# An attention and feed-forward kernel: output bias and three high halves on GpSimd in the last part, instead of bias matmuls and VectorE

## The reference

```
x = x + xattn(layernorm(x), ctx, ctx, wq, wk, wv, wo)     # 16 heads of 16: correlation by FFT over the
                                                          # head, the best lags, softmax, rolled v, @ wo
x = x + ffn(layernorm(x), W_in, b_in, W_out, b_out)

ffn:  W_in_sim  = W_in  rounded to 8 bits, a scale per column
      W_out_sim = W_out rounded to 8 bits, a scale per row
      x_sim     = x rounded to 16 bits, one scale for the whole tensor
      hidden    = gelu(x_sim @ W_in_sim + b_in)           # 1024 wide
      hidden_sim= hidden rounded to 16 bits, one scale for the whole tensor
      out       = hidden_sim @ W_out_sim + b_out
```

## Time and profile before

| | |
|---|---|
| median of the timed runs | 1077.34 us |
| the profiled execution | 1077.55 us, span 1075.8 us |
| TensorE busy | 1055.1 us, 98% |
| VectorE busy | 970.5 us, 90% |
| ScalarE busy | 936.8 us, 87% |
| GpSimd busy | 504.6 us, 47%, nearly all before 595 us |
| granted TensorE clock | 1.00 |

### The profile page before, as it was taken

The page is one execution under the profiler, slowest core; times in us unless marked ns, Lnnn a source line. Parts: engine busy times, 40 slices in busy tenths (PEclk is TensorE's granted clock), DMA queues, the critical chain, the costliest instruction groups (busy, mean ns, idle before and its releaser), DMA issues.

```text
span 1075.8 us, 29041 instructions
## 1 busy us (share of the span) xinstructions
PE 1055.1 (98%) x9358; PEld 779.8 (72%) x9358; DVE 970.5 (90%) x2798; ACT 936.8 (87%) x1697; POOL 504.6 (47%) x674
## 2 busy tenths in 40 slices
PE   9999999999999999999998999999999999999998
PEld 7788887887888888888886444444444888888886
DVE  4889989989889889889899999999997999999998
ACT  5888888998999998888888788888888999999996
POOL 5788887888888888888887300000000000000000
PEclk9999999999999999999999999999999999999999
DMA  5445343343444334334441499999989899999995
GB/s 167 129 149 143 120 119 119 119 119 119 119 128 130 119 119 120 119 119 119 119 126 43 167 313 312 313 303 300 300 303 372 323 342 329 353 335 351 337 344 198
DMA packets 141521, 222.59 MB, mean 207 GB/s; under 512 B 72416, under 2 KB 92256, under 8 KB 137312
## 3 DMA queue, kind: packets, MB, share of 16 engines
q1 hardware_dynamic: 140320, 220.12, 62.0%
q10 hardware_dynamic: 1088, 1.05, 0.3%
HBM read 121.00 MB, written 83.89 MB: 190 GB/s over the span
## 4 chain that ended last, share of the span: by engine, by line
PE 53%; DVE 11%; issue 8%; DMA 3%; ACT 2%; DVEq 1%; ACTq 0%; POOL 0%; SPq 0%; POOLq 0%
PE bank L612 21%; DVE arena L1482 6%; PE bank L441 5%; PE bank L454 5%; PE bank L492 4%; PE bank L516 4%; PE bank L466 3%; PE bank L504 3%; PE bank L478 3%; PE bank L533 3%; DMA arena<-x_scratch 2%; DVE arena L1475 2%; DVE arena L1497 2%; PE bank L643 1%; DMA out<-arena 1%
## 5 line engine op out<-in xcount | busy, mean ns | idle before, releaser
L643 PE MATMUL bank<-wout,arena 128*128 128x256 f16 x2048 | 235.5, 273 | 2.7 <-DVE arena L1475 0.7
L643 PEld LDWEIGHTS bank<-wout,arena 128*128 128x128 f16 x2048 | 195.7, 98 | 44.2 <-DVE arena L1482 13.2
L612 PE MATMUL bank<-arena,win 128*128 128x512 f16 x1024 | 221.3, 379 | 1.1 <-DVE arena L1430 0.9
L612 PEld LDWEIGHTS bank<-arena,win 128*128 128x128 f16 x1024 | 100.0, 98 | 122.4 <-issue 1.4
L1482 DVE SCALAR_TENSOR_TENSOR arena<-arena,wout_rel 128x512 f16<-128x512 int16 x256 | 183.0, 746 | 3.9 <-ACT arena L912 1.3
L869 ACT ACTIVATE arena<-bank,b_in_sb,z_scale 128x512 f32<-128x512 f32 x192 | 147.1, 778 | 15.1 <-PE bank L612 10.0
L733 ACT ACTIVATE arena<-arena 32x128 f32<-32x128 f32 x256 | 78.5, 307 | 52.7 <-DVE arena L1186 50.4
L663 ACT ACTIVATE arena<-bank 128x512 f32<-128x512 f32 (+1 forms) x196 | 115.4, 590 | 6.4 <-PE bank L441 3.0
L905 ACT ACTIVATE arena<-arena,one 128x1536 int16<-128x1536 f32 x64 | 100.2, 1568 | 17.5 <-DVE arena L1482 15.3
L663 ACT ACTIVATE arena<-arena 128x512 f16<-128x512 f32 x192 | 113.0, 618 | 1.5 <-POOL arena L972 0.9
L1449 DVE TENSOR_REDUCE hmax_all<-arena 128x1 f32<-128x1024 f32 x96 | 111.3, 1210 | 2.9 <-ACT arena L869 2.9
(11 more groups left out here) (130 smaller groups left out, 2057.3 us busy)
## 6 DMA issues: line engine op xcount, KB each, us to landing
hidden_scratch<-arena SPq DMA_DIRECT2D x32, 1536.0 KB, 5.5
arena<-hidden_scratch SPq DMA_DIRECT2D x64, 768.0 KB, 7.1
arena<-in_ctx_turned SPq DMA_DIRECT2D x64, 256.0 KB, 2.7
arena<-in_x_turned SPq DMA_DIRECT2D x64, 256.0 KB, 2.7
arena<-in_x SPq DMA_DIRECT2D x64, 256.0 KB, 3.6
x_scratch<-arena SPq DMA_DIRECT2D x64, 256.0 KB, 3.5
arena<-x_scratch SPq DMA_DIRECT2D x32, 512.0 KB, 6.2
out<-arena SPq DMA_DIRECT2D x32, 512.0 KB, 4.0
```

The lines of the kernel that those rows point to most:

```text
L612: last = nc.tensor.matmul(bank[f][:, :].rearrange("p (n t) -> p n t", n=4), win16[:, f, c, :], xt[q % 3][:, s, :, c, :], start=s == 0 and ...
L643: last = nc.tensor.matmul(bank[m * 2 + k // 2][:, k % 2 * D:(k % 2 + 1) * D], gbuf[:, s, f, k * P:(k + 1) * P], wout16[:, f, :], start=f = ...
```

## The change

- **Bias.** The two bias matmuls of each quad and all of GpSimd's preparation go (with a few columns of the constant table). GpSimd adds the bias itself to x1 once that is loaded: `add_bias(q)`, one addition over 128x1024 f32.
- **High halves.** GpSimd makes those of f = 2, 4 and 6, ScalarE those of 1, 3, 5 and 7, VectorE that of 0 alone. GpSimd's order in quad q is: high 2, add_bias(q-1), high 4, high 6.
- **Additions.** The two PSUM banks of a quad are declared as one tensor of 1024, and `finish` is one instruction after the rest of f = 4; for the last quad it is two, each with a store of its own. It waits for add_bias as well.
- **Third x1 buffer**, in room of `store_x` that the first part used. SyncE loads x1 of quad q+1 after the store of q-1 is issued. The loops on SyncE and VectorE are written out for all quads.
- **Scale chains.** The three dependent instructions of each weight's scale are put in three successive steps, and what follows them moves two steps later (ScalarE's `weights`, the transposition of W_in).

```diff
-HIGH_ON_ACT = (1, 3, 5, 6, 7)
-FINISH_AFTER = {4: 0, 6: 1}
+HIGH_ON_ACT = (1, 3, 5, 7)
+HIGH_ON_POOL = (2, 4, 6)
+FINISH_AFTER = 4
...
-        yq = cut(2, 1024, ("p (k) -> p k", {}))
+        yq = cut(2, 1024, ("p (k) -> p k", {})) + [store_x[:, 0:1024]]
...
+        sums = [ctx.enter_context(nc.psum_tensor(f"sums{n}", [P, 1024], F32)) for n in range(2)]
+        bank = [sums[n // 2][:, n % 2 * 512:n % 2 * 512 + 512] for n in range(4)]
...
-                    if f == FC - 1:
-                        pe.wait_ge(S["bias_ready"], 1)
-                        for j in range(2):
-                            last = nc.tensor.matmul(bank[m * 2 + j][:, :].rearrange("p (b d) -> p b d", b=2), y_rows, bias_rows.unsqueeze(1).broadcast_to([P, 2, D]),
-                                                    start=False, stop=True, skip_group_check=True)
...
+            bias = b_out_sb[:, :].unsqueeze(1).broadcast_to([P, 4, D])
+            def add_bias(q):
+                pool.wait_ge(s_x1_ld[q % 3], 16 * (q // 3 + 1))
+                y = yq[q % 3].rearrange("p (b d) -> p b d", b=4)
+                nc.gpsimd.tensor_tensor(y, y, bias, ALU.add).then_inc(S["y_biased"], 1)
+            def high(q, f):
...
+                pool.wait_ge(S["c_hq"], q * 3 + (sum(f >= b for _, b in PARTS_OF_F) + 1))
+                wait(pool, S["c_f"], (q - 1) * FC + (f + 1))
+                nc.gpsimd.tensor_scalar(gbuf[:, 0, f, :], hq[:, f, :], wout_rel[:, f:f + 1], None, ALU.mult).then_inc(S["c_hi_pool"], 1)
+            for q in range(QUADS):
+                for f in HIGH_ON_POOL[:1]:
+                    high(q, f)
+                if q > 0:
+                    add_bias(q - 1)
+                for f in HIGH_ON_POOL[1:]:
+                    high(q, f)
+            add_bias(QUADS - 1)
...
+            def finish(q, part, parts):
+                n = 1024 // parts
+                of = slice(part * n, (part + 1) * n)
+                dve.wait_ge(S["y_biased"], q + 1)
+                dve.wait_ge(S["c_f"], (q + 1) * FC)
+                V.scalar_tensor_tensor(yq[q % 3][:, of], sums[q % 2][:, of], y_scale, yq[q % 3][:, of],
+                                       ALU.mult, ALU.add).then_inc(S["c_out"], 1)
...
                 if n == FC:
-                    scales(win_max, win_up).then_inc(S["w_in_scaled"], 1)
+                    floor_w(win_max, FC)
+                if n == FC + 1:
+                    invert_w(win_max, win_up, FC + 1)
+                if n == FC + 2:
+                    scale_w(win_up, FC + 2).then_inc(S["w_in_scaled"], 1)
```

More of the change, by code:

```diff
@@ L41 @@
 C_TURN = C_HD + HD
-C_ROW = C_TURN + 1
-C_ALL = C_ROW + 6
+C_ALL = C_TURN + 1
 W_UP = 64.0
@@ L253, in xattn_ffn_kernel @@
         s_x1_st = [sem(f"s_x1_st{n}") for n in range(2)]
-        s_x1_ld = [sem(f"s_x1_ld{n}") for n in range(2)]
+        s_x1_ld = [sem(f"s_x1_ld{n}") for n in range(3)]
         s_h_st = [sem(f"s_h_st{n}") for n in range(2)]
@@ L257, in xattn_ffn_kernel @@
         s_xt = [sem(f"s_xt{n}") for n in range(3)]
-        s_out = [sem(f"s_out{n}") for n in range(2)]
+        s_out = [sem(f"s_out{n}") for n in range(3)]
         def wait(eng, s, n):
@@ L358, in load_hidden, with load_x1, store @@
                 sp.dma_start(hidden_in[n], rows(h_dram, q)[:, part * 1536:(part + 1) * 1536]).then_inc(s_h_ld[n], 16)
[L360 to L366, removed]
+            def load_x1(q):
+                wait(sp, s_out[q % 3], 16 * (q // 3))
+                sp.dma_start(yq[q % 3].rearrange("p (n k) -> p n k", n=2), x1_q[q]).then_inc(s_x1_ld[q % 3], 16)
+            def store(q):
+                sp.wait_ge(S["c_out"], q + 1)
+                sp.dma_start(out_q[q], yq[q % 3]).then_inc(s_out[q % 3], 16)
             def turn_x(q):
@@ L385, in _ @@
             sp.wait_ge(S["b_max"], QUADS * FC // 2)
[L386 to L406, removed]
+            for q in range(3):
+                load_x1(q)
+            for q in range(QUADS - 1):
+                if q + 2 < QUADS:
+                    for part in range(2):
+                        load_hidden(q + 2, q % 2, part)
+                if q > 0:
+                    store(q - 1)
+                if q > 1 and q + 1 < QUADS:
+                    load_x1(q + 1)
+            store(QUADS - 2)
+            last = QUADS - 1
+            for j in range(2):
+                sp.wait_ge(S["c_out"], QUADS + j)
+                sp.dma_start(out_q[last][:, j * 512:(j + 1) * 512], yq[last % 3][:, j * 512:(j + 1) * 512]).then_inc(s_out[last % 3], 16)
+            for m in range(3):
+                sp.wait_ge(s_out[m], 16 * ((QUADS + 2 - m) // 3 + (m == last % 3)))
         @block.tensor
@@ L921, in quad @@
                 high(q, 5)
-                high(q, 6)
                 high(q, 7)
@@ L1502, in _, with high @@
-            with dve.Fori(1, QUADS // 2) as i:
-                round_h(i * 2, 0)
-                round_h(i * 2 + 1, 1)
-            for j in range(2):
-                finish(QUADS - 1, 1, j)
+            def high(q, f):
+                if q == 0 and f == 0:
+                    dve.wait_ge(s_h_st[0], 16 * (QUADS // 2))
+                dve.wait_ge(S["c_hq"], q * 3 + (sum(f >= b for _, b in PARTS_OF_F) + 1))
+                wait(dve, S["c_f"], (q - 1) * FC + (f + 1))
+                V.tensor_scalar(gbuf[:, 0, f, :], hq[:, f, :], wout_rel[:, f:f + 1], None, ALU.mult).then_inc(S["c_hi_dve"], 1)
@@ L1509 @@
+            for q in range(QUADS):
+                high(q, 0)
+                for f in range(FC):
+                    if f + 1 < FC and f + 1 not in ELSEWHERE:
+                        high(q, f + 1)
+                    rest(q, f)
+                    if q > 0 and f == FINISH_AFTER:
+                        finish(q - 1, 0, 1)
+            for part in range(2):
+                finish(QUADS - 1, part, 2)
 _INS = ["x", "x_turned", "ctx_turned", "L0_xattn_wq", "L0_xattn_wk", "L0_xattn_wv", "L0_xattn_wo",
```

140 lines of the change are left out of this document (45 added, 95 removed).

## The result

| | before | after |
|---|---|---|
| median of the timed runs | 1077.2 us (1077.05 to 1078.33) | 1148.43 us (1146.67 to 1148.93) |
| the profiled execution | 1077.55 us, span 1075.8 us | 1148.29 us, span 1146.5 us |
| first rest of the last part | 824.88 us | 823.95 us |
| a round of the last part | 7.66 us | 9.92 us |

The ratio of after to before is 1.066 (95% interval 1.0637 to 1.0674). The forecast was 1143 us, between 1095 and 1200.

The account below looks back on a forecast made before the run. VectorE was taken to set the last part's pace, its round going from 7.67 to 6.9 + 2.9 = 9.8 us: 1077.3 + 68 - 1.6 - 0.4 = 1143 us, range 1095 to 1200.

Parts of the forecast that it names:

- GpSimd's high half: Last part, 128x512 int16 to f16 product on GpSimd: 1.1 us each, between 0.6 and 1.4; delays VectorE 0.6.
- paper round of 6.9 us: Last part, VectorE's round if GpSimd cost it nothing: 0.39 + 5.28 + 1.2 = 6.9 us.
- delay of 2.9 us a round: Last part, GpSimd holding up VectorE: 3 x 0.6 + 4 x 0.4 = 3.4 us, of which 2.9 counts.
- discount of 0.87: Last part, share of GpSimd's work that counts as delay; the rest falls beside addition L1497 or a wait, free.
- signs of being wrong: Last part: rests keeping 744 ns, or GpSimd's product over 512 values taking 2 us or more, its chain setting the round.
- GpSimd's chain: Last part, GpSimd's own work: 5.8 us a quad, some 7.5 us with waits, under 9.8, so not the bound.
- Rival A: Last part, no collision worth speaking of: round 7.3 us, the DMA engines' need, time 1063 us; 9 in 100.
- TensorE's need: Last part, TensorE without the two bias matmuls: 64 x 0.103 = 6.6 us a round.
- The first part: Scale chains spread to one step each: 1.6 us gained (0 to 2.4).
- rival B: Last part, partial collision of 0.8 to 1.7 us a round: round 7.7 to 8.6, 1077 to 1105 us; 8 in 100.
- rival C: Last part, GpSimd's four instructions hold VectorE up for their whole length: round 10.7 to 12 us, 1187 us; 20 in 100.
- Rival D: Last part, TensorE waits so often its clock falls to 1.2 GHz: round 13.2 us, 1252 us; 2 in 100.

Follow-up runs that it names:

- e5: e3 with GpSimd filling 128x512 f32 values five times a quad in room nothing reads; 1067.1 us, 0.991 of before.
- e6: e3 with one GpSimd addition over 128x1024 a quad, both inputs read from SBUF, result unused; 1089.8 us, 1.012 of before.
- e3: Changed kernel without output bias and with GpSimd idle in the last part (high halves 2, 4 on VectorE, 6 on ScalarE); 1066.9 us, 0.991 of before.
- e8: e4 with the 816-byte bias_room put behind all other SBUF buffers instead of ahead of them; full computation; 1067.4 us, 0.991 of before.
- e4: Changed kernel with output bias on TensorE again and high halves as before, bias_room ahead of store_x; 1075.4 us, 0.998 of before.
- e9: Kernel before with only 816 unused bytes a partition added ahead of store_x; 1082.4 us, 1.005 of before.
- e1: Changed kernel with GpSimd adding the bias but making no high halves (2, 4 on VectorE, 6 on ScalarE); 1130.1 us, 1.049 of before.

## Why the prediction was right

- **VectorE sets the pace of the last part, and GpSimd's reads are charged to it.** Shown by e5 and e6: fills cost a rest nothing, reads that nobody needs cost 0.7 us a round. The Trainium skill (SBUF — State Buffer, Who interferes with whom) is right here on who is held up: the rests with two SBUF inputs are, the addition with one input in PSUM isn't, and a write-only GpSimd instruction does nothing to a rest. Its "for the whole instruction" fits the bias addition (a delay of 2.09 in 2.41 us) and not GpSimd's high half: the one that began at 956.35 and ended at 958.91 delayed the rest of 957.47 by 0.36 us, and the next rest ran its usual 0.74 us from 958.5 on, while it still ran.
- **The paper round of 6.9 us.** Its parts were right: e3 has 7.42, which is 6.9 + 0.55 less 0.03. The two-bank addition costs 1.2 us from start to start (959.16 to 960.35), as estimated.
- **The delay of 2.9 us a round** measured 3.08, but two errors nearly cancel, and that is luck. The bias addition was priced at 1.6 us, by the 0.4 for 256 values; it is 2.09, most of the 2.41 us that it lasts. A high half was priced at 0.6. In the round shown the three cost 0.36, 0.63 (a rest by 0.43 and VectorE's high half by 0.2) and nothing beside the addition in PSUM: together 1.0 in place of 1.8. The discount of 0.87 for what lies beside that addition was the wrong form: it belongs to one instruction of the four, wholly.
- **GpSimd's high half** was taken to need 1.1 us alone, between 0.6 and 1.4. It needs 1.56: outside the bounds. This did no harm to the sum because most of that time doesn't exclude VectorE (a rest is delayed by 0.4 beside 1.56 us of work). Duration and exclusion are two numbers, and the forecast had tied them together. One of its signs of being wrong, a product of 2 us or more, was nearly met (the median is 1997 ns, waits included), and what it was to mean did not come: GpSimd's chain does not set the round.
- **GpSimd's chain isn't the bound**: it was busy 8.5 us of each 9.97 (183.85 of 215 us), more than the 7.5 forecast, yet VectorE waited for it once only (1.5 us in the first quad).
- **The best round.** Rival A's floor of 7.3 us, from the DMA engines, was not tested: in e3 and e8, with 7.42 and 7.41, VectorE's own work takes as long.
- **TensorE's need** was 6.6 us in the forecast, from the run of sixteen loads in the earlier trace rows. e3, which has no bias either, shows 64 loads behind a wait for VectorE, and e4, with the bias, 64 between the loads of two bias matmuls:

```profile
946.71 6.88 PEld L637 LDWEIGHTS sums<-wout,arena 128*128 128x128 f16 x64 [0.52 <-DVE arena L1466]
```

```profile
945.46 7.08 PEld L653 LDWEIGHTS sums<-wout,arena 128*128 128x128 f16 x64
...
952.55 0.21 PEld L659 LDWEIGHTS sums<-bias_room 128*128 128x128 bf16 x2
952.88 7.08 PEld L653 LDWEIGHTS sums<-wout,arena 128*128 128x128 f16 x64
```

So it is 6.9 us without the bias, and with it the whole 7.4 of a round (952.88 - 945.46): in e4 TensorE has no wait, and 24 loads are still to do at 1068.6, when VectorE's last rest is over. In e8 TensorE is as near to the bound as VectorE.
- **The first part** was to gain 1.6 us. The changed kernel's trace shows round_x 0.57 us earlier (596.03 instead of 596.60), but one trace of each can't tell: with the same chains the start of round_x lies anywhere from 593.8 to 597.3 us in the table above. The nine traces with the new chains have a mean of 595.2, the two with the old one (before, e9) of 596.8, a gain of 1.7 us, in accord with the forecast and not proof of it. The two stretches recovered 1.84 us of TensorE's time. The first round_x was 0.38 us shorter (596.03 to 597.89 against 596.60 to 598.84), as forecast (0.4), and the same 0.4 us stands between 227.9 and 228.3 in the table.
- **The end**: 2.5 us from the last addition's end to the span's end, against 3.1 before; e4, whose last addition is in two halves with a store each as well, has 2.5 too; bias addition 31 was done 3 us before it was needed.

The account: 32 x (9.92 - 7.66) = +72.2, -0.9 ahead of the last part, -0.6 at the end: +70.7 us, the difference of the two spans. Rival A failed by the long rests of the changed kernel and by e6, rival B because the delay was 3.1 us a round and not 0.8 to 1.7, rival C because a high half excludes for 0.4 us and not for its length. Rival D came in part, and cost nothing: two stretches of 10 us, in the columns of the earlier trace rows, show the granted clock at 1.00 and at 0.83.

```profile
904.00:914.00 10.00, 7.68 (x64) 5.88 (x64) 9.96 (x11) 6.75 (x7) 8.63 (x6) 1.00 0.72 258
914.00:924.00 10.00, 9.15 (x66) 7.04 (x67) 9.93 (x13) 7.57 (x8) 7.76 (x4) 0.83 0.76 279
```

TensorE had waited for over two of ten microseconds, and for a part of the second stretch it ran at 1.2 GHz. It did as many matmuls, busy for longer, and VectorE stayed busy throughout. Over the last part the mean is 0.96 to 0.97, and rounds kept the length that VectorE alone explains.

## What to carry to other kernels

Before work is moved to an idle GpSimd, look at what VectorE runs beside it: GpSimd's reads and VectorE's instructions with two SBUF inputs take turns, and VectorE's int16 product with one SBUF input was held up too (0.35 us became 0.55 to 0.78), so such work is not hidden but added to VectorE's time, and what it adds must be measured as delay, not read off GpSimd's duration. The delay shows as a longer busy time of the VectorE instruction, not as a wait. Work placed beside a VectorE instruction with one input in PSUM came free, and so did fills beside instructions with two SBUF inputs. And when a kernel gets slower in a part that wasn't edited, compare the landing times of its DMAs: a buffer added or taken out ahead of others moves them all.

## What the runs showed that was not expected

- The place of buffers in SBUF changed a transposing DMA's landing from 3.7 to 7.6 us (a shift of 816 bytes) or 4.5 us (a shift of 24 bytes the other way); with the first, the kernel before became 5.3 us slower (e9). Why is open.
- GpSimd's product of 512 int16 values with a column, to f16, takes 1.56 us, longer than its addition of 512 f32 values from two inputs (1.27 us), yet it holds a rest of VectorE up for about 0.4 us only, the addition over 1024 values for 2.1.
- A GpSimd instruction can be passed over: the one at 956.35 stood for a microsecond while rests of VectorE followed each other at their usual 0.66 us. The bias additions at 960.88 and, in e1, at 949.52 got in at the first change of instruction. What decides between the two wasn't found.
- The first part, the same instructions in the same order in nine kernels, ended anywhere within 3.5 us. A gain of 1 or 2 us there can't be read from one trace.
